# A fourth gathered head for batch 1 of each pair: 144 beats in place of 160

## What is computed

```python
def _pk(x, Wq_pk, pk_keys):
    q = (x @ Wq_pk).reshape(b, n, P, HEADS, DIM_KEY).transpose(2, 0, 1, 3, 4)
    sim = jnp.einsum('pbnhd,pkhd->pbnhk', q, pk_keys)      # 2 sides, 64 sub-keys each
    scores, idx = jax.lax.top_k(sim, 16)
    ...
    final_scores, pk_idx = jax.lax.top_k(score, 16)        # of the 16 x 16 sums
    final_indices = jnp.take_along_axis(index, pk_idx, axis=-1)
    final_scores = jax.nn.softmax(final_scores, axis=-1)
...
k = jnp.einsum('bnhk,bnhkd->bnhd', kv_scores, keys_table[ind])
v = jnp.einsum('bnhk,bnhkd->bnhd', kv_scores, values_table[ind])
```

## Time and profile before

| | |
|---|---|
| median of three runs | 11015.43 us (11011.72 to 11017.97) |
| the profiled execution: its time, its span | 11002.74 us, 11001.0 us |
| PE busy | 10047.6 us, 91% |
| DVE busy | 8710.8 us, 79% |
| ACT busy | 7763.9 us, 71% |
| POOL busy | 6309.3 us, 57% |
| granted PE clock, mean | 0.981 of 2.4 GHz |
| DMA | 1107.29 MB, 101 GB/s |

### The profile page before, as it was taken

One profiled execution on the slowest core, in us unless ns is written; L12 is line 12 of the kernel. 1 busy time (PEld: TensorE's weight loads), 2 busy tenths in 40 slices (PEclk: granted clock), 3 DMA queues, 4 the chain that ended last, 5 costly groups with the idle time before them and its releaser, 6 DMA issues.

```text
span 11001.0 us, 260917 instructions
## 1 busy us (share of the span) xinstructions
PE 10047.6 (91%) x72608; PEld 7627.2 (69%) x72608; DVE 8710.8 (79%) x41793; ACT 7763.9 (71%) x17491; POOL 6309.3 (57%) x6186
## 2 busy tenths in 40 slices
PE   5999989999999999999999999999999999999998
PEld 4766767767677676776776776676767767667666
DVE  7878778788787787887877878878778778787783
ACT  4777767777777777777777777777777777777775
POOL 5655556555555555555555555555555555555553
PEclk9999999999999999999999999999999999999998
DMA  2333333333333333333333333333333333333332
GB/s 77 104 103 102 101 100 104 102 100 105 101 103 102 101 103 102 101 103 102 102 102 101 104 101 99 105 102 102 101 103 103 102 100 104 102 102 101 102 103 71
DMA packets 603741, 1107.29 MB, mean 101 GB/s; under 512 B 158672, under 2 KB 175568, under 8 KB 602192
## 3 DMA queue, kind: packets, MB, share of 16 engines
q1 hardware_dynamic: 405328, 686.35, 20.4%
q0 software_dynamic: 196608, 403.05, 14.0%
q10 hardware_dynamic: 288, 0.27, 0.0%
HBM read 1084.90 MB, written 4.19 MB: 99 GB/s over the span
## 4 chain that ended last, share of the span: by engine, by line
PE 41%; DVE 34%; ACT 11%; issue 7%; DVEq 7%; POOL 0%; ACTq 0%; DMA 0%; POOLq 0%
PE p_d L1436 14%; DVE gath L943 5%; PE p_s L1423 4%; PE p_s L1414 4%; PE p_g L1378 4%; ACT ew L1174 3%; ACT prob L1242 3%; PE p_f L1362 2%; DVE rank_hot L915 2%; PE p_x L1586 2%; PE p_x L1579 2%; DVE cand L814 2%; ACT p_s L1169 1%; DVE idx_f L869 1%; DVE sim L853 1%
## 5 line engine op out<-in xcount | busy, mean ns | idle before, releaser
L654 POOL DMA_INDIRECT gath<-in_table,idx x6144 | 6285.1, 1023 | 4574.1 <-PE p_d L1436 3538.7
L1436 PE MATMUL p_d<-ew,tab 128*128 128x256 f32 x20480 | 6241.5, 387 | 0.9 <-ACT dense_t_sb L1180 0.8
L1174 ACT ACTIVATE ew<-p_s 128x512 f32<-128x512 f32 x5120 | 3089.1, 603 | 1302.8 <-PE p_s L1423 1223.1
L1169 ACT ACTIVATE p_s<-p_s 128x512 f32<-128x512 f32 x5120 | 3060.5, 598 | 1196.5 <-PE p_s L1414 1135.7
L1436 PEld LDWEIGHTS p_d<-ew,tab 128*128 128x128 f32 x20480 | 3146.5, 194 | 157.3 <-issue 22.5
L1423 PE MATMUL p_s<-mov,piece_sel 128*128 128x256 f16 x10240 | 1987.4, 276 | 163.6 <-ACT p_s L1169 163.6
L1414 PE MATMUL p_s<-mov,rank_sel 128*128 128x256 f16 x10240 | 1984.5, 276 | 60.5 <-issue 31.0
L1414 PEld LDWEIGHTS p_s<-mov,rank_sel 128*128 128x128 f16 x10240 | 959.4, 100 | 871.5 <-ACT ew L1174 234.0
L1423 PEld LDWEIGHTS p_s<-mov,piece_sel 128*128 128x128 f16 x10240 | 934.8, 99 | 809.9 <-ACT p_s L1169 250.1
L943 DVE SCALAR_TENSOR_TENSOR gath<-gath,kv_w 128x128 f32<-128x128 f32 x4608 | 1307.8, 345 | 64.2
L915 DVE TENSOR_TENSOR rank_hot<-iota_k,rank_key 128x2048 f16<-128x2048 f16 x640 | 776.8, 1222 | 84.1 <-issue 71.5
(11 more groups left out here) (238 smaller groups left out, 12242.9 us busy)
## 6 DMA issues: line engine op xcount, KB each, us to landing
tab<-in_dense_t SPq DMA_DIRECT2D x2560, 256.0 KB
gath<-in_table,idx POOLq DMA_INDIRECT x6144
xin<-in_x SPq DMA_DIRECT2D x64, 128.0 KB, 2.2
out<-h_out SPq DMA_DIRECT2D x64, 64.0 KB, 1.7
row_consts<-in_rows SPq DMA_DIRECT2D x1, 548.0 KB, 4.2
w_sb<-in_w SPq DMA_DIRECT2D x1, 512.0 KB, 5.9
w_sb<-in_w ACTq DMA_DIRECT2D x1, 256.0 KB, 4.5
gath<-in_wqpk_t SPq DMA_DIRECT2D x1, 256.0 KB, 5.4
```

The source lines that it names most:

```text
L654: G.indirect_dma_start(out=gath[:, slot, k, :], out_offset=None, in_=table[:, :], in_offset=bass.IndirectOffsetOnAxis(ap=idx[pair.par][:, ...
L1169: A.activation(bank[:, :], bank[:, :], ACT.Relu, scale=-STEEP).then_inc(penalty_ready, 1)
L1174: A.activation(ew[:, slot:slot + 2, :].rearrange("m c t -> m (c t)"), p_s[u % PS_RING][:, :], ACT.Exp, scale=-1.0).then_inc(weights_ready, 1)
L1436: M(p_d[:, 0:2 * T], tab[:, u % TAB_RING, i, :], ew[:, c % EW_RING, :], start=(k == 0), stop=(k == CHUNKS - 1)).then_inc(product_done, 1)
```

## The change

The two batches of a pair no longer gather the same heads. Batch 0 gathers heads 0 to 2 as before, batch 1 heads 0 to 3 (`GATHERED_OF = (3, 4)`): 7 sets of 16 rows in a pair, which take the slots 0, 1, 2, 3, 0, 1, 2 of a ring of four. Head 3, the first dense one (`d = 0`), is dense for batch 0 alone (`batches_of`). Its matmuls have 128 columns, and since two chunks then fit where one did, it takes 16 beats (`HALF_HEAD`), with two products to a beat and four chunks to a unit (`unit`). A pair has 144 beats. The other four heads are as they were. All due times that are spread over `BEATS` are pressed into 144, gathers are due every 144/112 = 1.29 beats, and `mov` of heads 0 and 1 gets due times of its own (`FIRST_FILL_AT`, `SECOND_FILL_AT`): it is now filled for head 1 before the first step of `select`, and not after it. The tables' bytes are unchanged: all five dense tables are still read whole. The one-hot search for batch 1 has 64 row numbers in place of 48.

The core of the diff:

```diff
 DENSE = 5
-GATHERED = HEADS - DENSE
-PICKS = GATHERED * TOPK
+FIRST_DENSE = HEADS - DENSE
+GATHERED_OF = (FIRST_DENSE, FIRST_DENSE + 1)
+ROW_SETS = [(p, h) for p in range(2) for h in range(GATHERED_OF[p])]
+SETS = len(ROW_SETS)
+PICKS = max(GATHERED_OF) * TOPK
 CHUNKS = SUBKEYS * SUBKEYS // 128
-BEATS = DENSE * CHUNKS
+HALF_HEAD = CHUNKS // 2
+BEATS = HALF_HEAD + (DENSE - 1) * CHUNKS
+RANKED = 2 * DENSE - 1
 HALF = SUBKEYS // 2
...
 PER_LAYOUT = CHUNKS // LAYOUTS
 QUAD = 4
-QUADS = BEATS // QUAD
+QUADS = DENSE * CHUNKS // QUAD
 TAB_RING = 4
...
 PRODUCT_AT = 0.9
-RING = 3
+RING = 4
 MOV_RING = 2 + DENSE % 2
 HALF_TABLE = SUBKEYS * SUBKEYS // 2
...
 
+def head_start(d):
+
+    return HALF_HEAD + CHUNKS * (d - 1) if d else 0
+
+
+def batches_of(d):
+
+    return (0, 1) if d else (0,)
+
+
+def quad_end(u):
+
+    return 2 * u + 2 if u < 8 else HALF_HEAD + QUAD * (u - 7)
+
+
+def ranked(d, p):
+
+    return 2 * d + p if d else 1
+
...
 UNITS_END = SELECT_AT + 0.4 * BEATS
-SELECT_END = CHUNKS * (DENSE - 1) + 4
+SELECT_END = head_start(DENSE - 1) + 10
 SELECT_US = 66.0
 UNIT_US = 9.35
...
 
-    return CHUNKS * ((d - 1) % DENSE) + LAG + beat
+    return head_start((d - 1) % DENSE) + LAG + beat
 
 
 
 FILLS = ((0, 1), (1, 3), (3, 5))
 FILL_AT = (0.25, 6.25, 8.25)
-FIRST_FILL_AT = (5.25, 8.25, 10.25)
+SECOND_FILL_AT = (-5.75, -1.75, 1.25)
+FIRST_FILL_AT = (11.25, 14.25, 16.25)
 
 
 def at_fill(d, part):
-    return at_prep(d, (FILL_AT if d > 0 else FIRST_FILL_AT)[part])
+    return at_prep(d, (FIRST_FILL_AT, SECOND_FILL_AT, FILL_AT)[min(d, 2)][part])
 
...
 
-GATHER_STEP = BEATS / (2 * GATHERED * TOPK)
+GATHER_STEP = BEATS / (SETS * TOPK)
...
 
-    ready = CHUNKS * (d + 1) + LAG
+    ready = head_start(d + 1) + LAG
...
     onehot = scratch[:, _at:_at + PICKS * CANDP].rearrange("t (k c) -> t k c", c=CANDP)
-    half_hot = onehot[:, :, 0:CANDP // 2]
     idx_f = sb("idx_f", [T, PICKS])
     idx = [sb(f"idx{p}", [T, 2, PICKS], I32) for p in range(2)]
 
 
     below = sb("below", [T, DENSE, SUBKEYS])
     pieces = [sb(f"pieces{p}", [T, 2, DENSE, 2, SIDES, 2, HALF], F16) for p in range(2)]
-    _at += PICKS * CANDP
...
                 d, q = divmod(u, CHUNKS // QUAD)
-                free = QUADS * pair.n + u - TAB_RING + 1
+                last = u - TAB_RING
+                free = BEATS * pair.n + quad_end(last) if last >= 0 else BEATS * (pair.n - 1) + quad_end(last + QUADS)
                 if positive(free):
-                    hold(sp, product_done, QUAD * free)
+                    hold(sp, product_done, free)
...
         def gather(pair):
-            for m in range(2 * GATHERED):
-                p, h = divmod(m, GATHERED)
+            for m, (p, h) in enumerate(ROW_SETS):
                 if h == 0:
                     yield at_gather(m, 0) - 0.2
                     hold(pool, idx_ready, 2 * pair.n + p + 1)
-                if positive(2 * GATHERED * pair.n + m - RING + 1):
+                last = m - RING if m >= RING else max(k for k in range(SETS) if k % RING == m) - SETS
+                if positive(SETS * pair.n + last + 1):
                     yield at_gather(m, 0) - 0.1
-                    hold(pool, summed, 2 * GATHERED * pair.n + m - RING + 1)
-                slot = (2 * GATHERED * pair.par + m) % RING
+                    hold(pool, summed, SETS * pair.n + last + 1)
+                slot = m % RING
                 for k in range(TOPK):
...
             for p in range(2):
-                for h in range(GATHERED):
+                for h in range(GATHERED_OF[p]):
                     g = HEADS * p + h
...
             for p in range(2):
-                mine = slice(HEADS * p, HEADS * p + GATHERED)
+                heads = GATHERED_OF[p]
+                picks = heads * TOPK
+                mine = slice(HEADS * p, HEADS * p + heads)
+                hot = onehot[:, 0:picks, :]
+                half_hot = hot[:, :, 0:CANDP // 2]
                 yield at_select(50.6 + 4.7 * p)
-                V.tensor_copy(pos_h[:, :, :],
+                V.tensor_copy(pos_h[:, 0:picks, :],
...
                                 iota_c[:, :].rearrange("t (c i) -> t c i", i=2)[:, None, :, :]
-                                .to_broadcast([T, PICKS, CANDP // 2, 2]),
-                                pos_h[:, :, None, :].to_broadcast([T, PICKS, CANDP // 2, 2]), ALU.is_equal)
+                                .to_broadcast([T, picks, CANDP // 2, 2]),
+                                pos_h[:, 0:picks, None, :].to_broadcast([T, picks, CANDP // 2, 2]), ALU.is_equal)
                 V_sync()
                 yield at_select(52.1 + 4.7 * p)
...
@@ -928,9 +956,8 @@
                 yield from prepare(pair, d)
 
         def weigh(pair):
-            for m in range(2 * GATHERED):
-                p, h = divmod(m, GATHERED)
-                rows = gath[:, (2 * GATHERED * pair.par + m) % RING, :, :]
+            for m, (p, h) in enumerate(ROW_SETS):
+                rows = gath[:, m % RING, :, :]
                 share = kv_w[pair.par][:, HEADS * p + h, :]
                 yield at_weigh(m)
                 dve.wait_ge(gathered[pair.par][m], 16 * TOPK * pair.half + 16 * TOPK)
...
                 act.wait_ge(map_tr, 3 * DENSE * pair.n + 3 * d + part + 1)
-                into = mov[mov_slot(d)][:, first:last, :].rearrange("q a t -> q (a t)")
+                width = T * len(batches_of(d))
+                into = mov[mov_slot(d)][:, first:last, 0:width]
+                made = p_g[:, 0:2 * T * (last - first)].rearrange("q (a t) -> q a t", t=2 * T)[:, :, 0:width]
                 if part == 0:
-                    A.activation(into, p_g[:, 0:2 * T], ACT.Identity, bias=rank_off[:, 0:1]).then_inc(bank_free, 1)
+                    A.activation(into[:, 0, :], made[:, 0, :], ACT.Identity, bias=rank_off[:, 0:1]).then_inc(bank_free, 1)
                 else:
-                    A.copy(into, p_g[:, 0:2 * T * (last - first)]).then_inc(bank_free, 1)
+                    A.copy(into, made).then_inc(bank_free, 1)
 
         def prep(pair):
             for d in range(1, DENSE):
...
                     at = 2 * T * half + T * p
                     last = M(p_g[:, at:at + T], pieces[pair.par][:, p, d, half, :, :, :].rearrange("t s w i -> t (s w i)"),
                              ident_h[:, :], start=True, stop=True)
...
 
+        def unit(u):
+
+            if 2 * u < HALF_HEAD:
+                return 0, T, range(4 * u, 4 * u + 4)
+            d, k = divmod(2 * u - HALF_HEAD, CHUNKS)
+            return d + 1, 2 * T, range(k, k + 2)
+
         def ranks(pair, u):
-            d, k = divmod(2 * u, CHUNKS)
-            if k == 0:
+            d, width, chunks = unit(u)
+            if chunks[0] == 0:
                 pe.wait_ge(bank_free, bank_use(pair, "map", 3 * d + 2) + 1)
             last_user = u - PS_RING if u >= PS_RING else max(k for k in range(TWOS) if k % PS_RING == u) - TWOS
             if positive(TWOS * pair.n + last_user + 1):
                 pe.wait_ge(weights_ready, TWOS * pair.n + last_user + 1)
-            for i in range(2):
-                last = M(p_s[u % PS_RING][:, 2 * T * i:2 * T * i + 2 * T], rank_sel[:, k + i, :], mov[mov_slot(d)][:, 0, :],
-                         start=(i == 0), stop=False, skip_group_check=True)
+            for i, k in enumerate(chunks):
+                last = M(p_s[u % PS_RING][:, width * i:width * i + width], rank_sel[:, k, :],
+                         mov[mov_slot(d)][:, 0, 0:width], start=(i == 0), stop=False, skip_group_check=True)
             last.then_inc(ranks_mm, 1)
 
         def exponents(pair, u):
-            d, k = divmod(2 * u, CHUNKS)
-            layout, k = divmod(k, PER_LAYOUT)
+            d, width, chunks = unit(u)
             pe.wait_ge(penalty_ready, TWOS * pair.n + u + 1)
-            for i in range(2):
-                last = M(p_s[u % PS_RING][:, 2 * T * i:2 * T * i + 2 * T], piece_sel[:, k + i, :],
-                         mov[mov_slot(d)][:, MAP_OF[layout], :], start=False, stop=True, skip_group_check=True)
+            for i, k in enumerate(chunks):
+                last = M(p_s[u % PS_RING][:, width * i:width * i + width], piece_sel[:, k % PER_LAYOUT, :],
+                         mov[mov_slot(d)][:, MAP_OF[k // PER_LAYOUT], 0:width], start=False, stop=True,
+                         skip_group_check=True)
             last.then_inc(exponents_mm, 1)
 
         def product(pair, c):
-            d, k = divmod(c, CHUNKS)
-            u, i = divmod(c, QUAD)
+            d, width, chunks = unit(c // 2)
+            chunks = chunks[0:2] if d == 0 and c % 2 == 0 else chunks[2:4] if d == 0 else chunks[c % 2:c % 2 + 1]
+            k = chunks[0]
+            u, i = divmod(CHUNKS * d + k, QUAD)
             if i == 0:
                 pe.wait_ge(tab_loaded[u % TAB_RING], 16 * (QUADS // TAB_RING) * pair.n + 16 * (u // TAB_RING) + 16)
-            if i % 2 == 0:
+            if c % 2 == 0:
                 pe.wait_ge(weights_ready, TWOS * pair.n + c // 2 + 1)
```

(4 more changed lines are left out.)

78 lines of the change are left out of this document (40 added, 38 removed).

## The result

The changed kernel takes 11068.58 us in the median of 5 runs (11057.41 to 11074.64), the kernel before 11015.43 us on the same chip (5 runs, 11011.72 to 11020.17). The ratio is 1.0048, 95% interval 1.0037 to 1.006. I had predicted 10925 us and faster. The profiled execution has a span of 11060.4 us.

What follows compares the result with a forecast made beforehand. PE and DVE were taken to bound the kernel alternately. 48.6 + 85.2 + 33.8 + 0.3 = 167.9 us a pair against 169.2, with PE's 10 us in full in the last period, gave 10925 us, range 10790 to 11120.

Steps and rivals of the forecast that it cites:

- Period by stretches, which engine sets which: A 169.2 us pair in three stretches: PE's order sets the first and third, DVE the second; DVE becomes the first's limit.
- Stretch 1, 48.6: From DVE's first maximum of `select` to the fourth step's: from 47.6 to 48.6 us, the three DVE waits gone.
- DVE's work, net +5.6 us a pair: All DVE work: a seventh set, larger one-hot search and more index searches, less one `rank_hot` write and its product.
- PE's work, -11.6 us a pair: All PE work: 16 beats (10.4 us), 16 rank matmuls (about 0.9), halved pieces and transposes (some 0.3) saved.
- Stretch 2, 85.2: From the fourth `select` step's maximum to PE's first transpose of `xh1`: from 85.4 to 85.2 us, set by DVE.
- between 0 and 1.5, I take 0.7: Likely new wait in us a pair between `attn_o` and `h2`, with some 5.5 us of DVE work there instead of 10.
- Stretch 3, 33.8: From PE's first transpose of `xh1` to the next pair's first maximum: from 36.2 to 33.8 us, PE's order setting it.
- PE's saved beats buy nothing here, since PE waits: Between the fourth `select` step's maximum and PE's first `xh1` transpose, PE's saving was priced at nothing.
- Gathers, 0.3 us a pair: Allowance for a gathered set that lands late now and then.
- the third rival: Late gathers at a pair's last set, 3 us a pair, 11110 us; sign: DVE row waits over 2 us a pair; chance 0.2.
- The new order of stretch 3: `fill(1)` waiting for two one-hot writes: nothing, up to 2 us if missed; earlier Gelu block: -1.7 to +0.5, taken as -0.8.
- The fourth rival: Pressed chains bring new waits, or half-width matmuls cost 2.5 us uncovered: 2 us a pair, 11050 us; chance 0.1.

Runs made afterwards that it cites:

- experiment 1: Changed kernel with `h2` due 2.6 beats later on DVE alone, nothing left out: 10944.5 us, 0.994 of the kernel before.
- 3: Changed kernel without the weighing of ranks 4 to 15 of the fifth gathered set, so part of the attention is left out: 10893.7 us, 0.9894 of the kernel before.
- experiment 8: Changed kernel with unread matmuls in PE's waits, 32 ahead of `xn` and 16 ahead of `xh1` at the gram: 11000.6 us, 0.9991 of the kernel before.
- experiment 2: Changed kernel with each gather held for PE's product six beats sooner, nothing left out: 11040.7 us, 1.0032 of the kernel before.
- experiment 4: Changed kernel with 48 unread matmuls ahead of PE's wait for `xn` only: 11129.7 us, 1.0108 of the kernel before.

## Why the prediction was wrong

I forecast 1.3 us a pair less and it was 0.8 more. Two steps failed: the size of the new wait ahead of `h2`, and PE's longer waits, which I priced at nothing and which cost clock in a chain that DVE waits for. Point by point:

- *Period by stretches, which engine sets which*: right. The edits move the stretch that they should (1 and 3 stretch 2, 8 stretch 3), and stretch 1 never moves.
- *Stretch 1, 48.6*: right, 48.5 in the mean. DVE starts the second, third and fourth maximum at 5076.98, 5092.57 and 5108.90 with no wait for `sim`. The trace also prices the half-width units: from one L1451 to the next, 5066.38 to 5067.83 us, is 1.45 us, and 1.30 for a wide one as before, so eight cost at most some 1.2 us more, near the 1 us that I took. They fall under DVE's work as I said. But PE is busy 46.05 of 48.40 us where I had counted 43.4, so the cover was about half of what I thought.
- *DVE's work, net +5.6 us a pair*: right, (9061.2 - 8710.8) / 64 = 5.5.
- *PE's work, -11.6 us a pair*: its busy time fell by (10047.6 - 9649.9) / 64 = 6.2. Part of the rest is the same work at a lower clock: with the clock kept up PE has 9929.9 us, 48 x 64 matmuls without use among them, some 8.1 us a pair by the two rows of 5.36 and 2.76 us, so about 9410 without. That is 10 us a pair less than before, and up to 1.2 of the 1.6 that are missing are the half-width units. This term was near.
- *Stretch 2, 85.2*: wrong by half a microsecond in its length and by 1.0 against the mean of before. The step that failed is "between 0 and 1.5, I take 0.7": the new wait ahead of `h2` measures 2.2 us a pair, and experiment 1, with the wait filled, shows what it is worth, 1.5 us of the stretch. That is twice what I took and the very end of my bounds. Another 0.3 us of the stretch stays open. I had compared DVE's work between `attn_o` and `h2` with PE's and ACT's operations one after the other, and left out what stands between them in their queues. In the trace ACT's copy of the transposes (L1283) starts only behind a penalty (L1198) that itself waits 0.95 us for PE, and PE's `wo` behind four piece transposes (L1418) that wait 0.45 us for ACT. That these gaps make the wait is read from one pair's trace, and no run takes them out.
- *Stretch 3, 33.8*: its floor is right, 33.9 to 34.0 us in most pairs with the clock up. That it is the mean was wrong. The step that failed is the one that I never took: I wrote "PE's saved beats buy nothing here, since PE waits" of stretch 2, and priced the longer waits at nothing. They are not free. Where PE stood 1.9 us or more for `xh1` its clock fell in 26 of 30 pairs, and the gram's chain, on which DVE waits, took up to 2.8 us longer: 1.0 us a pair in the mean, by experiment 8 worth 68 us. I had also read the stretch from one pair (36.2 us, where the mean is 36.8), and so left out the one pair in four that is longer; the change made it 0.3 us a pair dearer, and no run shows why.
- *Gathers, 0.3 us a pair*: not borne out. What experiment 2 gained, 0.2 to 0.3 us in the period, is no more than what the gram's chain lost in it (0.35). A gather took POOL 1.04 us in the mean, 1.02 before. My own sign for the third rival (over 2 us of waiting a pair) was met, 154.1 / 64 = 2.4, and yet the rival fails, in place and in price: a wait's length isn't its worth when another stands right behind it.
- *The new order of stretch 3* (`fill(1)` behind two one-hot writes, the Gelu block): PE waits 14.7 us in all at L1408, so nothing, as said.
- *The fourth rival*, new waits of 2 us a pair, 11050 us, had a chance of 0.1. It is the one that came nearest. Its mechanism was too vague to be read as a forecast: one new wait is real, the clock is no part of it. That 11068.6 us lies within my range at all is luck: its upper end, 11120, was there for the third rival, which fails.

The sum with the measured terms: -1.3 us as forecast, +0.8 for the wait at `h2` (1.5 in place of 0.7), +1.0 for the clock, +0.3 for the one pair in four, is the 0.8 that was measured. Smaller errors cancel in it: +0.3 in stretch 2 and -0.2 in the other two.

Left open: why the clock did not fall in 4 of the 30 pairs with a long wait at the gram (2.50 us in one of the pairs above, against 2.44 in the other), why it comes back behind `xn` sooner in some pairs than in others, and what it would cost to keep it up without matmuls that nobody reads.

## What to carry to other kernels

When an edit takes work off TensorE in a stretch that another engine sets, the saved time turns into waiting, and the waiting was not neutral here: look in the trace for the chain of small matmuls behind the wait on which another engine stands, and price it at both clocks. The mean clock did not tell; it rose in a slower kernel. Nor is a wait's length its price, and a gain as small as 28 us can come from another place than the edit's: compare the stretches too. And when a schedule is pressed into fewer beats, walk each round trip through all queues on it, because a gap that another engine's program order makes is as real as an operation.

## What I had not expected of the hardware

- In the gram's chain the same 56 matmuls and their waits took 10.27 us at a granted clock of 1.00 and 13.04 at 0.78; two fp32 matmuls of the product 0.60 and 1.06 us, fp16 ones with 256 columns 0.38 and 0.63.
- A low clock can shield: in the 23 pairs of the changed kernel in which the clock behind `xn` stayed low for longer (0.59 to 0.64 in the mean up to the gram) PE did not wait at the gram and no chain ran low; in the 30 with 0.79 to 0.88 it waited 1.9 us or more and 26 did.
- The fall moves. PE kept busy in a wait of 6 us had its clock fall in one of 2.9 us that followed (experiment 4), at a place where it cost 61 us more.
- Matmuls of bf16 with 256 columns had a pitch of 5.40 / 48 = 0.11 us and with 384 columns 5.36 / 32 = 0.17 us.
